# The image stage of a one-layer vision tower: side work in another order, decay references added by GpSimd, one exponential per slot

## The chip, the cores and the metric

The kernel runs on one core of a Trainium2 chip. The metric is the device time of one execution in microseconds. The time before is the median of three runs.

## What is computed

Sixteen images of 5x128x128 are cut into 256 patches each. A patch embedding (320 to 256) with a normalisation gives the tokens h; a gated decay attention with 16 heads of 64 adds to h; a mixture of 8 experts, two per token, adds again. The part that the change touches is the decay of the attention and the order of what is done beside it:

```
q, k = silu(x Wq), silu(x Wk);  v = x Wv;  gate = sigmoid(x Wg)
cum   = cumsum(-softplus(x Wa + ba), over the tokens of an image)
decay = exp(where(causal, cum_i - cum_j, -inf))        per head
o     = ((q k^T) * decay) v;  o = norm(o per head) * gn_w + gn_b
h     = h + (o * gate) Wo;    then norm, router, top 2, experts
```

## The kernel before, in words

The image stage works on pairs of images: eight pairs (p), and for each eight steps (c), one for every two heads. The five engines each have a program written out by hand, and `step(p, c)` of each lists what it does in that step. Besides the attention of pair p ("main"), a step holds side work of the neighbours: the embedding of pair p+1 ("nxt": `tokens`, `embed`, `embed_norm`, `turn`, `keep_xnT`, `decay_logits`, `softplus`, `log_decay`, `cum`, `running_sums`, `keep_cum`), the second half of the output projection and the second normalisation of pair p-1 ("post": `gn_mean`, `spread`, `gn_var`, `affine`, `affined`, `gated`, `y_hi`, `y_lo`, `out_proj`, `residual`, `normed`, `turn2`, `keep_x2`, `route`), and the sorting of pair p-2 into lists by expert ("routed": `choose`, `ranks`, `place`, `scatter`). Engines take their instructions strictly in the order written; semaphores join them.

The main work of a step on TensorE is: `scores` of image 0 (L883, L886), `queries` of the next step (L849), `weighted` of image 0 (L896, L900), `scores` of image 1, `keys` and `gates` of the next step (L849), `weighted` of image 1; the eight blocks of v are made by `values` (L842), spread over the steps. `gates(4)` waits until all eight blocks of v have been copied out of their PSUM banks by ScalarE's `keep_v` (L585). The last step of a pair also has the first half of the output projection (`out_proj`, L926).

Decay. The running sums are written to HBM and read back, broadcast to 128 partitions, into a ring of four slots (`dec_x`, 128x768 each: two heads of 384 columns; a slot is one image of one step). SyncE loads a slot (`load_decay`) when VectorE has used the slot four before it. GpSimd's `decay_rows` (L449) fills what is not causal with -1e30, one step ahead of its use; ScalarE's `decay` (L594) takes exp with the negative running sum `ncum` as the bias of a partition: four instructions a slot, because the bias differs by head and by block of rows. VectorE's `decayed` (L1197) multiplies the scores with it. GpSimd's other work is reciprocal roots by pow (`embed_rsqrt` L455, `group_rsqrt` L460, `row_rsqrt` L464) and `scatter`, eight indirect DMAs a pair (L471), four in step 3 and four in step 4. In `decay_rows` order before, a root or four indirect DMAs stand between the slot of image 0 and that of image 1.

After the image stage comes the expert stage: 39 blocks of 256 rows, whose code is not touched.

Of the kernel before, what the change touches and what calls it, by code (L numbers as in the profile page):

```python
# [65 lines left out]
def vit_layer(nc, xT, w_tok, gamma, wq, wk, wv, wg, wa, ba, wo, gn_w, gn_b,  # L66
# [3 lines left out]
    with ExitStack() as ctx:  # L70
# [88 lines left out]
        st = sb("st", [P, NS, 3])  # L159
        rs = sb("rs", [P, NS])  # L160
# [61 lines left out]
        dec_in0 dec_in1 dec_in2 dec_in3 causal exp_done  # L222
# [41 lines left out]
        def _(sp):  # L264
# [70 lines left out]
            for p in range(NPR):  # L335
                for c in range(NP):
                    if c == 6 and pair(p + 1):
                        store_cum(p + 1)
                    ahead(p, c, 0)
                    if pair(p + 1):  # L340
                        if c == 0:
                            load_patches(2 * p + 3)
# [4 lines left out]
                    if c == 2 and pair(p + 2):  # L347
# [85 lines left out]
        def _(pool):  # L433
# [9 lines left out]
            def decay_rows(p, c, u):  # L443

                n = 2 * NP * p + 2 * c + u
                pool.wait_ge(M[f"dec_in{n % RING}"], 16 * (n // RING + 1))
                for hh in range(2):
# [14 lines left out]
            def row_rsqrt(n):  # L462
                pool.wait_ge(M["b_ve"], n + 1)
                pool.tensor_tensor(rs[:, :], rs[:, :], mhalf[:, 0:NS], ALU.pow).then_inc(M["b_rs"], 1)  # L464
# [9 lines left out]
            for p in SPAN:  # L474
                for c in range(NP):
                    nc_p, nc_c = (p, c + 1) if c + 1 < NP else (p + 1, 0)
                    if pair(nc_p):
                        decay_rows(nc_p, nc_c, 0)
                    if c == 0 and pair(p + 1):
                        embed_rsqrt(2 * p + 2)  # L480
                    if c == 2 and pair(p + 1):
                        embed_rsqrt(2 * p + 3)
                    if c in (3, 4) and pair(p - 2):
                        scatter(p - 2, c - 3)
                    if c in (4, 5) and pair(p - 1):
                        row_rsqrt(2 * p - 2 + c - 4)
                    if pair(nc_p):
                        decay_rows(nc_p, nc_c, 1)
                    if c == 0 and pair(p - 1):
                        group_rsqrt(2 * p - 1)  # L490
                    if c == 5 and pair(p):
                        group_rsqrt(2 * p)
# [30 lines left out]
        def _(act):  # L523
# [63 lines left out]
            def decay(p, c, u):  # L587
                n = 2 * NP * p + 2 * c + u
                act.wait_ge(M["causal"], 2 * (n + 1))
                act.wait_ge(M["ncum_done"], p + 1)  # L590
                for hh in range(2):
                    for s, cols in ((0, slice(0, S)), (1, slice(S, LW))):
                        d = dec[n % RING][:, hh, cols]
                        act.activation(d, d, ACT.Exp, bias=ncum[p % 2][:, NS * u + s, 2 * c + hh:2 * c + hh + 1]).then_inc(M["exp_done"], 1)  # L594
# [32 lines left out]

            def step(p, c):
                main, nxt, post, routed = pair(p), pair(p + 1), pair(p - 1), pair(p - 2)
                if c == 7 and nxt:  # L630
                    xn_hi(p + 1)
                if main and c > 0:
                    keep_o(p, c - 1)
                if main and c + 1 < NP:
                    tanh_q(p, c + 1)
                    decay(p, c + 1, 0)
                if main:
                    if c == 0:
                        keep_v(p, 2, 2)
                        keep_v(p, 3, 1)  # L640
                    if c == 1:
                        keep_v(p, 4, 2)
                if nxt and c == 1:
                    keep_xnT(2 * p + 2)
                if post and c == 1:
                    affined(p - 1, 1, 0)
                if post and c == 2:
                    affined(p - 1, 1, 1)
                if main and c == 2:
                    keep_v(p, 6, 2)  # L650
                if main and c == 3:
                    keep_v(p, 7, 2)
                if post and c == 3:
                    y_hi(p - 1, 1, 1)
                if main and c == 6:
                    affined(p, 0, 0)
                if nxt and c == 6:
                    keep_cum(p + 1)
                if main and c + 1 < NP:
                    tanh_k(p, c + 1)  # L660
                if post and c == 6:
                    keep_x2(2 * p - 2)
                if main and c == 1:
                    keep_v(p, 5, 0)
                if main and c + 1 < NP:
                    decay(p, c + 1, 1)
                if main and c == 6:
                    affined(p, 0, 1)
                if nxt and c == 4:
                    softplus(p + 1)  # L670
                if main and c + 1 < NP:
                    tanh_g(p, c + 1)
                if nxt and c == 1:
                    scaled_h(2 * p + 2)
                if nxt and c == 3:
                    scaled_h(2 * p + 3)
                    keep_xnT(2 * p + 3)
                if routed and c == 1:
                    top_exp(2 * p - 4)
                    top_exp(2 * p - 3)  # L680
                if post and c == 2:
                    y_hi(p - 1, 1, 0)
                if post and c == 6:
                    keep_x2(2 * p - 1)
                if c == 7:
                    if nxt:
                        decay(p + 1, 0, 0)
                        tanh_q(p + 1, 0)
                        keep_v(p + 1, 0, 2)
                    if main:  # L690
                        y_hi(p, 0, 0)
                        keep_o(p, 7)
                    if nxt:
                        tanh_k(p + 1, 0)
                        keep_v(p + 1, 1, 0)
                    if main:
                        y_hi(p, 0, 1)
                    if nxt:
                        decay(p + 1, 0, 1)
                        tanh_g(p + 1, 0)  # L700
# [89 lines left out]
        def _(pe):  # L790
# [62 lines left out]
            def queries(p, c):  # L853
# [4 lines left out]
                have(pe, "v_done", 2 * TP * p + {1: 2, 3: 6}.get(c, 0))  # L858
# [9 lines left out]
            def gates(p, c):  # L868
# [3 lines left out]
                have(pe, "v_done", 2 * TP * p + {0: 1, 1: 3, 2: 5, 3: 7, 4: 8}.get(c, 0))  # L872
# [31 lines left out]
            def gn_mean(p, g):  # L904
                n = 2 * p + g
                have(pe, "h2a_done", 2 * p + 2 if g == 1 else 0)
                have(pe, "h2_done", 2 * p - 1 if g == 0 else 0)
# [3 lines left out]
            def gn_var(p, g):  # L911
                n = 2 * p + g
                have(pe, "h2_done", 2 * p if g == 0 else 0)
# [45 lines left out]
            def step(p, c):  # L959
                main, nxt, post, routed = pair(p), pair(p + 1), pair(p - 1), pair(p - 2)  # L960
                if main:
                    scores(p, c, 0)
                    if c + 1 < NP:
                        queries(p, c + 1)
                if main:
                    if c == 0:
                        values(p, 2, 2, "tg_done", NP * p + 1)
                        values(p, 3, 1, "sk_done", NP * p + 1)
                    if c == 1:
                        values(p, 4, 2, "tg_done", NP * p + 2)  # L970
                    if c == 2:
                        values(p, 6, 2, "tg_done", NP * p + 3)
                    if c == 3:
                        values(p, 7, 2, "tg_done", NP * p + 4)
                if c == 0 and post:
                    gn_mean(p - 1, 1)
                if c == 1 and nxt:
                    turn(2 * p + 2)
                if c == 3 and nxt:
                    turn(2 * p + 3)  # L980
                if c == 4 and nxt:
                    logits(p + 1)
                if c == 4 and post:
                    out_proj(p - 1, 1, 0, *(("taken_done", p - 1) if routed else ("gv_done", 2 * p)))
                if c == 5 and post:
                    out_proj(p - 1, 1, 1, *(("gt2_done", 2 * p + 1) if main else ("h2_done", 2 * p - 1)))
                if c == 6 and nxt:
                    cum_rows(p + 1)
                if c == 6 and post:
                    turn2(2 * p - 2, *(("gv_done", 2 * p + 1) if main else ("h2_done", 2 * p)))  # L990
                if c == 7:
                    if pair(p + 2):
                        tokens(2 * p + 4)
                    if post:
                        route(2 * p - 1)
                if main:
                    weighted(p, c, 0)
                    scores(p, c, 1)
                    if c + 1 < NP:
                        keys(p, c + 1)  # L1000
                if c == 0 and post:
                    gn_var(p - 1, 1)
                if c == 1:
                    if main:
# [590 lines left out]
```

## Time and profile before

| what | us |
|---|---|
| median of 3 runs (lowest, highest) | 1525.53 (1521.51, 1531.65) |
| the profiled execution's own time | 1527.12 |
| its span in the trace | 1525.3 |
| image stage in steady work, 48 to 970 us of the span | 922 |
| expert stage, from 1030 us | 495 |

The profile is of one execution. Busy times of an engine are unions of its instructions; a mean duration of a matmul holds its latency, so the time that a group of matmuls takes is read from the starts in the timeline.

### The profile page before, as it was taken

How to read it: one execution, taken by the hardware profiler on the slowest of the kernel's cores; microseconds unless marked ns; L12 is line 12 of the kernel's file. 1: busy time of each engine (PE TensorE's matmuls, PEld its weight loads, DVE VectorE, ACT ScalarE, POOL GpSimd, SP SyncE). 2: the span in 40 equal slices, each digit the busy share in tenths (PEclk: the TensorE clock that was granted, in tenths of full speed). 3: DMA queues.
4: the chain of work that ended last, by engine and by line, in shares of the span. 5: the costliest groups of instructions: out<-in, count | busy, mean ns of one | idle time of the engine just before them, and what ended most of it. 6: DMA issues, size and time to landing. Idle time of an engine off the chain costs nothing. (4 is left out here: it accounts for less than half of the span.)

```text
span 1525.3 us, 28980 instructions
## 1 busy us (share of the span) xinstructions
PE 1347.0 (88%) x9012; PEld 1132.2 (74%) x9012; DVE 923.7 (61%) x2290; ACT 933.9 (61%) x2197; POOL 462.0 (30%) x538
## 2 busy tenths in 40 slices
PE   4799899889889988989888899437999999999996
PEld 3566666667667766767767777437999999999996
DVE  3445454554554564465455555555888888888884
ACT  2557456456366365464555575306888888888884
POOL 2111112132132133124023223131444444444544
PEclk9999999999999999999999999658999999999999
DMA  5322123132132222223222223227777777777772
GB/s 188 95 71 103 50 85 92 50 103 82 61 94 70 82 79 83 83 68 105 70 70 97 74 84 98 76 75 240 218 224 216 221 227 238 230 233 220 214 228 61
DMA packets 126021, 192.86 MB, mean 126 GB/s; under 512 B 17216, under 2 KB 92192, under 8 KB 125792
## 3 DMA queue, kind: packets, MB, share of 16 engines
q1 hardware_dynamic: 111344, 174.52, 35.3%
q0 software_dynamic: 14592, 17.26, 5.2%
q8 instruction: 46, 0.75, 0.2%
q14 instruction: 39, 0.32, 0.1%
HBM read 166.01 MB, written 29.96 MB: 128 GB/s over the span
## 5 line engine op out<-in xcount | busy, mean ns | idle before, releaser
L849 PE MATMUL bank<-xn_sp,big_r 128*128 128x512 f32 x1152 | 316.6, 412 | 0.0
L594 ACT ACTIVATE dec_x<-dec_x,ncum 128x256 f32<-128x256 f32 (+1 forms) x512 | 190.2, 446 | 134.4 <-POOL dec_x L449 134.4
L849 PEld LDWEIGHTS bank<-xn_sp,big_r 128*128 128x128 f32 x1152 | 204.5, 190 | 55.2 <-issue 4.5
L1197 DVE TENSOR_TENSOR att<-bank,dec_x 128x384 f32<-128x384 f32 x256 | 130.7, 552 | 186.5 <-PE bank L886 176.4
L1073 PE MATMUL bank<-big_r 128*128 128x256 f32 x1872 | 239.0, 284 | 0.9 <-DVE big_r L1487 0.9
L1073 PEld LDWEIGHTS bank<-big_r 128*128 128x128 f32 x1872 | 231.9, 193 | 1.3 <-DVE big_r L1487 1.3
L1437 DVE TENSOR_TENSOR big_r<-big_f,big_r 128x512 fp32r<-128x512 f32 x236 | 162.6, 691 | 12.8
L743 ACT ACTIVATE mid_f<-bank,dec_x 128x256 f32<-128x256 f32 x312 | 145.0, 477 | 27.4 <-DVE big_r L1505 23.0
L502 POOL TENSOR_SCALAR mid_f<-mid_f,dec_x 128x256 f32<-128x256 f32 x78 | 91.0, 1172 | 227.0 <-DVE mid_f L1513 227.0
L1505 DVE TENSOR_TENSOR big_r<-mid_f,big_r 128x256 fp32r<-128x256 f32 x312 | 131.7, 422 | 39.5 <-ACT big_r L749 39.5
L449 POOL TENSOR_SCALAR_AFFINE_SELECT dec_x<-dec_x 128x256 f32<-128x256 f32 x256 | 103.7, 437 | 156.2 <-DMA dec_x<-cum_scratch 156.1
L729 ACT ACTIVATE big_r<-big_f 128x512 fp32r<-128x512 f32 x236 | 149.4, 636 | 0.0
L926 PE MATMUL bank<-big_r,y_sp 128*128 128x256 f32 x768 | 119.8, 323 | 33.2 <-DVE y_sp L1245 31.6
L926 PEld LDWEIGHTS bank<-big_r,y_sp 128*128 128x128 f32 x768 | 116.3, 231 | 38.0 <-issue 34.7
L508 POOL DMA_INDIRECT out<-mid_f,tok x78 | 128.4, 1646 | 47.7 <-POOL mid_f L502 30.6
L455 POOL TENSOR_TENSOR rs<-rs,mhalf 128x4 f32<-128x4 f32 x16 | 23.7, 1481 | 360.4 <-DVE rs L1132 360.4
L749 ACT ACTIVATE big_r<-mid_f 128x256 fp32r<-128x256 f32 x312 | 132.6, 425 | 0.0
L1085 PE MATMUL bank<-big_r 128*128 128x256 f32 x960 | 124.4, 286 | 0.0
L1085 PEld LDWEIGHTS bank<-big_r 128*128 128x128 f32 x960 | 119.2, 194 | 0.0
L1085 PE MATMUL bank<-y_sp,big_r 128*128 128x256 f32 x912 | 117.1, 285 | 0.0
L842 PE MATMUL bank<-big_r,xn_sp 128*128 128x512 f32 x384 | 100.2, 401 | 18.3 <-ACT big_f L578 18.3
L1085 PEld LDWEIGHTS bank<-y_sp,big_r 128*128 128x128 f32 x912 | 111.9, 192 | 0.0
(154 smaller groups left out, 1990.2 us busy)
## 6 DMA issues: line engine op xcount, KB each, us to landing
big_f<-in_L_ffn_w SPq DMA_DIRECT2D x78, 1024.0 KB, 6.5
dec_x<-cum_scratch SPq DMA_DIRECT2D x128, 384.0 KB, 3.5
mid_f<-expert_rows SPq DMA_DIRECT2D x39, 261.0 KB, 7.0
tq<-in_L_ffn_b SPq DMA_DIRECT2D x39, 128.0 KB, 2.9
xt<-in_x SPq DMA_DIRECT2D x16, 256.0 KB, 3.8
h_scratch<-h SPq DMA_DIRECT2D x16, 256.0 KB
h<-h_scratch SPq DMA_DIRECT2D x8, 512.0 KB, 4.3
out<-h SPq DMA_DIRECT2D x16, 256.0 KB, 4.0
```

What stands on the lines that cost most here:

```text
L508: pool.indirect_dma_start(out=out_rows, out_offset=bass.IndirectOffsetOnAxis(ap=tok[par][:, s:s + 1], axis=0), in_=yo[par][:, s, :], in_of ...
L594: act.activation(d, d, ACT.Exp, bias=ncum[p % 2][:, NS * u + s, 2 * c + hh:2 * c + hh + 1]).then_inc(M["exp_done"], 1)
L729: act.activation(parts[0].rearrange("p k n -> p (k n)")[:, cols], staged[par][:, cols], ACT.Copy).then_inc(M[f"{name}_hi"], 1)
L743: act.activation(gel[c % NGEL], bank[2 + c % HB][:, 0:BLK], ACT.Gelu_apprx_tanh, bias=b1_sb[par][:, c:c + 1]).then_inc(M["gel_done"], 1)
L749: act.activation(g_sp[0][:, c, :], gel[c % NGEL], ACT.Copy).then_inc(M["gh_done"], 1)
L849: mm = pe.matmul(bank[target][:, :], wp[:, k, c * P:(c + 1) * P], xp[:, k, :], start=(k == 0 and j == 0), stop=(k == EC - 1 and j == 2))
L926: mm = pe.matmul(bank[7][:, s * E:(s + 1) * E], yp[:, j, u * S + s * P:u * S + (s + 1) * P], wp[:, GC * g + j, :], start=(j == 0 and s == ...
L1073: mm = pe.matmul(bank[2 + c % HB][:, 0:BLK], wp[:, k, c * P:(c + 1) * P], xp[:, k, :], start=(k == 0 and j == 0), stop=(k == EC - 1 and j ...
L1085: mm = pe.matmul(bank[6 + s // 2][:, (s % 2) * E:(s % 2 + 1) * E], gp[:, c, s * P:(s + 1) * P], wp[:, c, :], start=(c == 0 and s % 2 == 0 ...
L1197: dve.tensor_tensor(att[hh][:, :], bank[4 + hh][:, 0:LW], dec[n % RING][:, hh, :], ALU.mult).then_inc(M["mult_done"], 1)
L1437: dve.tensor_tensor(lo, staged[par][:, cols], f32(hi), ALU.subtract).then_inc(M[f"{name}_lo"], 1)
L1505: dve.tensor_tensor(g_sp[1][:, c, :], gel[c % NGEL], f32(g_sp[0][:, c, :]), ALU.subtract).then_inc(M["gl_done"], 1)
```

## The change

It reorders the side work of all five engines' steps and moves the subtraction of the running sums from ScalarE's bias to GpSimd. The diff, cut to what the prediction speaks of:

```diff
 GpSimd
-            pool.wait_ge(dec_in); two affine_selects
+                pool.wait_ge(M["ncum_done"], p + 1)
+                for s, cols in ((0, slice(0, S)), (1, slice(S, LW))):
+                    d = dec[n % RING][:, :, cols]
+                    ref = ncum[p % 2][:, NS * u + s, 2 * c:2 * c + 2].rearrange(...).broadcast_to(d.shape)
+                    pool.tensor_tensor(d, d, ref, ALU.add).then_inc(M["shifted"], 1)
+                pool.wait_ge(M["shifted"], 2 * (n + 1))
...
+                    q, d = (p, c + 1) if c + 1 < NP else (p + 1, 0)
+                    if pair(q):
+                        decay_rows(q, d, 0)
+                        decay_rows(q, d, 1)
+                    if c == 0 and post:
+                        group_rsqrt(2 * p - 1)
+                    if c in (0, 2) and nxt:
+                        embed_rsqrt(2 * p + 2 + c // 2)
+                    if c in (2, 3) and routed:
+                        scatter(p - 2, c - 2)
+                    if c in (4, 5) and post:
                         row_rsqrt(2 * p - 2 + c - 4)
+                    if c == 5 and main:
                         group_rsqrt(2 * p)
 ScalarE
-                for hh in range(2):
-                    for s, cols in ((0, slice(0, S)), (1, slice(S, LW))):
-                        d = dec[n % RING][:, hh, cols]
-                        act.activation(d, d, ACT.Exp, bias=ncum[...]).then_inc(M["exp_done"], 1)
+                d = dec[n % RING].rearrange("p h n -> p (h n)")
+                act.activation(d, d, ACT.Exp).then_inc(M["exp_done"], 1)
 SyncE
                 for c in range(NP):
-                    if c == 6 and pair(p + 1):
-                        store_cum(p + 1)
-                    ahead(p, c, 0)
...
+                        if c == 2: store_h(2 * p + 2)
+                        if c == 4: store_h(2 * p + 3)
+                        if c == 6: store_cum(p + 1)
+                    ahead(p, c, 0)
```

The new order, by step (the instructions themselves stay, except as above):

- TensorE: step 0 `values` 2 and 3, `gn_mean`, `gn_var`; step 1 `values` 4, `ranks`, `turn`, `values` 5; step 2 `tokens(2p+3)` (was step 1), `values` 6 into bank 0 behind `keys` (was bank 2 behind `queries`); step 3 `values` 7, and `turn(2p+3)` behind `gates` (was ahead of `weighted`); step 4 `out_proj(p-1,1,0)` , `logits` behind `keys`, `out_proj(p-1,1,1)` behind `gates` (was step 5); step 5 `gn_mean(p,0)`, `gn_var(p,0)`, `turn2(2p-2)` (was step 6); step 6 `cum` (was step 5), `route(2p-2)`, `turn2(2p-1)`, `cum_rows`, `route(2p-1)` (was step 7); step 7 both `out_proj(p,0,.)` one behind the other at the end (a `gates` stood between them).
- ScalarE: `softplus` in step 5 (was 4); `keep_cum` first in step 7 (was step 6); `keep_xnT(2p+3)` at the head of step 4 (was the end of step 3); `keep_x2(2p-2)` at the head of step 6; in step 3 the order is `keep_o`, `tanh_q(4)`, `decay(4,0)`, `keep_v(7)`, `y_hi(p-1,1,1)`, `tanh_k(4)`, `decay(4,1)`, `scaled_h`, `tanh_g(4)`; in step 7 `decay(p+1,0,0)` stands behind `tanh_q` and `keep_v`.
- VectorE: in step 2 `decayed(2,0)`, `head_stats`, `silu_q(3)`, `place`, `decayed(2,1)`, `silu_k(3)`, `gated(p-1,1,1)`, `embed(2p+3)` (was near the head of step 2); `embed_norm(2p+3)` behind `silu_k(4)` in step 3; `residual(2p-1)` and both halves of `normed` a little earlier in the steps; `gated(p,0,0)` in step 6 (was 7) and `gated(p,0,1)` early in step 7.
- `rs` and `st` get two buffers, so that the rows of one image need not wait for the other.

## Rows read from the trace of the kernel before

**Rows 1.** The page, part 1: busy us, share of span, instructions.

```profile
PE 1347.0 (88%) x9012; PEld 1132.2 (74%) x9012; DVE 923.7 (61%) x2290; ACT 933.9 (61%) x2197; POOL 462.0 (30%) x538
```

**Rows 2.** Windows: stretch, length, busy of PE, PEld, DVE, ACT, POOL, clock, DMA.

```profile
48.00:970.00 922.00, 828.82 (x4944) 627.92 (x4943) 478.20 (x1196) 503.15 (x1135) 213.21 (x347) 0.96 0.26 83
1030.00:1525.00 495.00, 473.34 (x3900) 470.14 (x3900) 394.83 (x928) 399.14 (x1007) 219.38 (x156) 0.98 0.71 213
```

**Rows 3.** Waits of PE, 48 to 970 us: us in total, times, longest.

```profile
PE bank L926 <- DVE y_sp L1245: 24.8, 8, 3.9
PE bank L842 <- ACT big_f L578: 18.3, 7, 3.3
PE bank L896 <- DVE att L1197: 16.1, 13, 2.8
PE bank L818 <- ACT xs L530: 14.0, 5, 2.8
PE bank L944 <- ACT turned L618: 9.5, 7, 1.4
```

**Rows 4.** Waits of ACT, same stretch.

```profile
ACT dec_x L594 <- POOL dec_x L449: 134.4, 42, 6.2
```

**Rows 5.** Timeline of POOL in pair 3: start us, us, instructions [idle before].

```profile
413.05 1.01 POOL L455 TENSOR_TENSOR rs<-rs,mhalf 128x4 f32<-128x4 f32 x1 [30.14 <-DVE rs L1132]
...
439.22 1.93 POOL L455 TENSOR_TENSOR rs<-rs,mhalf 128x4 f32<-128x4 f32 x1 [20.57 <-DVE rs L1132]
...
447.07 1.03 POOL L471 DMA_INDIRECT expert_rows<-xn,slot  x1 [4.47 <-DVE slot L1330]
...
453.91 1.48 POOL L449 TENSOR_SCALAR_AFFINE_SELECT dec_x<-dec_x 128x256 f32<-128x256 f32 x4
```

**Rows 6.** Timeline of PE in pair 3.

```profile
423.60 3.34 PE L802 MATMUL bank<-wt,xt 128*128 128x256 f32 x12
...
428.45 0.65 PE L896 MATMUL bank<-att,mid_f 128*64 128x256 f32 x4
...
429.25 0.70 PE L883 MATMUL bank<-q_s,k_s 64*128 64x256 f32 x4
...
430.11 1.67 PE L849 MATMUL bank<-xn_sp,big_r 128*128 128x512 f32 x6
...
459.83 4.61 PE L926 MATMUL bank<-big_r,y_sp 128*128 128x256 f32 x24
...
472.85 3.03 PE L926 MATMUL bank<-big_r,y_sp 128*128 128x256 f32 x24
```

**Rows 7.** Groups by line and shape, whole span: busy us, mean ns, idle before.

```profile
L594 ACT ACTIVATE dec_x<-dec_x,ncum 128x256 f32<-128x256 f32 x256 | 128.4, 501 | 134.4 <-POOL dec_x L449 134.4
...
L449 POOL TENSOR_SCALAR_AFFINE_SELECT dec_x<-dec_x 128x256 f32<-128x256 f32 x256 | 103.7, 437 | 156.2 <-DMA dec_x<-cum_scratch 156.1
L594 ACT ACTIVATE dec_x<-dec_x,ncum 128x128 f32<-128x128 f32 x256 | 100.1, 391 | 0.0
L502 POOL TENSOR_SCALAR mid_f<-mid_f,dec_x 128x256 f32<-128x256 f32 x78 | 91.0, 1172 | 227.0 <-DVE mid_f L1513 227.0
...
L471 POOL DMA_INDIRECT expert_rows<-xn,slot x64 | 73.8, 1153 | 70.0 <-DVE slot L1330 53.8 <-issue 16.2
...
L571 ACT ACTIVATE tq<-bank 128x512 f32<-128x512 f32 x64 | 38.2, 596 | 118.1 <-PE bank L849 118.0
...
L612 ACT ACTIVATE y_sp<-big_f 128x1024 fp32r<-128x1024 f32 x32 | 33.6, 1050 | 4.4 <-DVE big_f L1239 4.4
```

**Rows 8.** Timeline of DVE in pair 3, an `embed` and what follows it.

```profile
436.43 0.70 DVE L1119 BATCH_NORM_STATS2 st<-bank 128x6 f32<-128x512 f32 x1 [3.30 <-DMA h_scratch<-h]
...
439.06 1.23 DVE L1239 SCALAR_TENSOR_TENSOR big_f<-big_f 128x1024 f32<-128x1024 f32 x1
...
441.14 0.68 DVE L1188 SCALAR_TENSOR_TENSOR k_s<-tq,bank 128x512 f32<-128x512 f32 x1
...
442.18 0.88 DVE L1140 TENSOR_SCALAR turned<-h,st1u,rs 128x256 f32<-128x256 f32 x2
```

More of the change, by code:

```diff
@@ L346, in _ @@
                             store_h(2 * p + 3)
-                    if c == 2 and pair(p + 2):
+                        if c == 6:
+                            store_cum(p + 1)
+                    ahead(p, c, 0)
+                    if c == 0 and pair(p + 1):
+                        load_patches(2 * p + 3)
+                    if c == 3 and pair(p + 2):
                         load_patches(2 * p + 4)
@@ L626, in top_exp, with last_step @@
                                    accum_out=tsum[:, t, :]).then_inc(M["tope_done"], 1)
+            def last_step(p):
+                main, nxt = pair(p), pair(p + 1)
+                if nxt:
+                    keep_cum(p + 1)
+                    xn_hi(p + 1)
+                if main:
+                    y_hi(p, 0, 0)
+                    keep_o(p, 6)
+                    y_hi(p, 0, 1)
+                if nxt:
+                    tanh_q(p + 1, 0)
+                    keep_v(p + 1, 0, 2)
+                    decay(p + 1, 0, 0)
+                if main:
+                    keep_o(p, 7)
+                if nxt:
+                    tanh_k(p + 1, 0)
+                    keep_v(p + 1, 1, 0)
+                    decay(p + 1, 0, 1)
+                    tanh_g(p + 1, 0)
@@ L635, in step @@
+                if main:
                     tanh_q(p, c + 1)
                     decay(p, c + 1, 0)
-                if main:
[L638 to L648, printed above, removed]
@@ L678, in step @@
-                if routed and c == 1:
+                    for i, source in {0: ((2, 2), (3, 1)), 1: ((4, 2),), 3: ((7, 2),)}.get(c, ()):
+                        keep_v(p, i, source)
+                if c in (1, 2) and post:
+                    affined(p - 1, 1, c - 1)
+                if c == 3 and post:
+                    y_hi(p - 1, 1, 1)
+                if c == 5 and nxt:
+                    softplus(p + 1)
+                if c == 6 and main:
+                    affined(p, 0, 0)
+                if main:
+                    tanh_k(p, c + 1)
@@ L679, in step @@
+                if c == 6 and post:
+                    keep_x2(2 * p - 1)
+                if main:
+                    decay(p, c + 1, 1)
+                    if c in (1, 2):
+                        keep_v(p, c + 4, 0)
+                if c == 0 and routed:
                     top_exp(2 * p - 4)
                     top_exp(2 * p - 3)
-                if post and c == 2:
+                if c == 1 and nxt:
+                    keep_xnT(2 * p + 2)
+                    scaled_h(2 * p + 2)
+                if c == 2 and post:
@@ L682, in step @@
                     y_hi(p - 1, 1, 0)
[L683 to L700, printed above, removed]
+                if c == 3 and nxt:
+                    scaled_h(2 * p + 3)
@@ L702, in start @@
+                if c == 6 and main:
+                    affined(p, 0, 1)
+                if main:
+                    tanh_g(p, c + 1)
             def start(c):
@@ L906, in gn_mean @@
                 have(pe, "h2a_done", 2 * p + 2 if g == 1 else 0)
-                have(pe, "h2_done", 2 * p - 1 if g == 0 else 0)
+                have(pe, "h2_done", 2 * p if g == 0 else 0)
                 pe.wait_ge(M["gst_done"], GC * (n + 1))
@@ L957, in ranks, with last_step @@
                 mm.then_inc(M["rk_ps"], 1)
-            def step(p, c):
-                main, nxt, post, routed = pair(p), pair(p + 1), pair(p - 1), pair(p - 2)
+            def last_step(p):
+                main, nxt = pair(p), pair(p + 1)
                 if main:
-                    scores(p, c, 0)
-                    if c + 1 < NP:
-                        queries(p, c + 1)
+                    scores(p, 7, 0)
+                if pair(p + 2):
+                    tokens(2 * p + 4)
                 if main:
[L966 to L1004, printed above, removed]
-                        values(p, 5, 0, "sq_done", NP * p + 3)
-                    if nxt:
-                        tokens(2 * p + 3)
-                if c == 2 and routed:
-                    ranks(p - 2, *(("gv_done", 2 * p) if post else ("taken_done", p - 2)))
-                if c == 4 and main:
-                    gn_mean(p, 0)
-                if c == 5:
-                    if main:
-                        gn_var(p, 0)
-                    if nxt:
-                        cum(p + 1)
-                if c == 6 and post:
-                    route(2 * p - 2)
-                if main and c + 1 < NP:
-                    gates(p, c + 1)
-                if c == 6 and post:
-                    turn2(2 * p - 1, "lg_done", 2 * p - 1)
-                if c < 7:
-                    if main:
-                        weighted(p, c, 1)
-                    return
@@ L1027, in step @@
+                    weighted(p, 7, 0)
+                    scores(p, 7, 1)
                 if nxt:
@@ L1331, in place, with last_step @@
                                          op0=ALU.mult, op1=ALU.add).then_inc(M["slot_done"], 1)
+            def last_step(p):
+                main, nxt, post = pair(p), pair(p + 1), pair(p - 1)
+                if main:
+                    decayed(p, 7, 0)
+                if post:
+                    keep_logits(2 * p - 1)
+                if main:
+                    gated(p, 0, 1)
+                if nxt:
+                    xn_lo(p + 1)
+                if main:
+                    head_stats(p, 6)
+                    y_lo(p, 0, 0)
+                    decayed(p, 7, 1)
+                if nxt:
+                    silu_q(p + 1, 0)
+                if main:
+                    y_lo(p, 0, 1)
+                if nxt:
+                    silu_k(p + 1, 0)
+                if post:
+                    choose(2 * p - 2)
+                if main:
+                    first_half(p, 0)
+                    first_half(p, 1)
@@ L1369, in step @@
-                if main and c == 7:
-                    gated(p, 0, 0)
+                if c == 2 and routed:
+                    place(p - 2)
+                if c == 3 and post:
+                    y_lo(p - 1, 1, 0)
+                if c == 5:
+                    if post:
+                        normed(2 * p - 2)
+                    if main:
+                        spread(p, 0)
+                if c == 6:
+                    if post:
+                        normed(2 * p - 1)
+                        keep_logits(2 * p - 2)
+                    if nxt:
+                        running_sums(p + 1)
```

250 lines of the change are left out of this document (124 added, 126 removed).

## The prediction, made before the changed kernel was run

> **What bounds the kernel now.** I read the page first, then the windows by stage, the waits of TensorE in the image stage, and then one pair (pair 3, 394 to 510 us) instruction by instruction. The page shows TensorE busy for 88% of the span, twice as long as GpSimd and well ahead of VectorE and ScalarE at 61% [rows 1]. The windows split this: the expert stage is 96% busy on TensorE (473.34 of 495 us) and is not touched; the image stage has 922 us with TensorE busy for 828.82 [rows 2]. So 93 us of idle time, about 12 us in each of eight pairs of 115.3 us, is all that a better order can win at the present speed of the matmuls. The waits name it: five of them hold 82.7 us [rows 3]. ScalarE and VectorE are busy for 55% and 52% of this stage [rows 2], so for them it is only lateness that counts, not length.
>
> Where the lateness comes from: ScalarE stands 134.4 us before the exponential, waiting for GpSimd's causal fill [rows 4]. GpSimd is late because its queue stands behind something else: at 439.22 it had waited 20.57 us for an `embed` before it could go on to the fill of image 1, and at 447 to 454 us four indirect DMAs stood between two fills [rows 5].
>
> **The change, part by part.** Times are on the clock of TensorE, from the start of a step. From the starts in the trace: `weighted` 0.80, `scores` 0.86, one projection or block of v 1.5, `tokens` 3.3, an `out_proj` 3.0 us at full clock [rows 6]; ScalarE 0.60 for 512 columns, 1.05 for 1024 [rows 7]; VectorE 1.2 for `gated`, 2.6 from the start of `embed` to its last statistic, 0.7 for a silu, 0.8 for `embed_norm` [rows 8].
>
> Exponential. Four instructions of 2x501 and 2x391 ns are 1.78 us of durations for a slot; one of 768 columns without bias lies between 596 ns for 512 and 1050 for 1024 columns, so 0.82 us [rows 7]. For 128 slots that is 123 us less on ScalarE. ScalarE is 45% idle, so I count nothing for it by itself: the matmuls hide it. If the cover is gone, it is worth 1 us wherever ScalarE is what is late.
>
> GpSimd's additions: 128x512 and 128x256 for a slot. The trace has no such instruction. The fill costs 437 ns for 256 columns, so three times that, 1.3 us, is the low end; L502, one operation of arithmetic on 256 columns, costs 1172 ns, so 3.5 us is the high end [rows 7]. I take 2.4 us, midway, as two instructions carry less fixed cost than three. With the two fills a slot then costs 3.2 us, and two slots 6.4 of a step of 14.4 on average. GpSimd's load rises by 16 x 2.4 = 38 us a pair, to 65 of 115 us (27 now [rows 2]): not a bound, but it matters wherever GpSimd starts late.
> The Trainium skill (GPSIMD Engine Reference, Elementwise — side-by-side cycle accounting) gives about 2.6 cycles of 1.2 GHz a column for an addition of two tensors, by which the additions would be 1.7 us a slot, and the stall below 0.7 us shorter. No run here shows it yet.
>
> Order, what goes. `gated(p,0,0)` moves from step 7 to 6, so the second `y_lo` is ready before `out_proj`: the 24.8 us go; both `out_proj` now stand next to each other, and the second waits some 0.9 us for `first_half` (0.7 us and the signals), 7 us in eight pairs. Both fills precede the roots, so `tanh_g` of step 0 is not late for `values(4)`: the 18.3 us go. `store_h` is issued before a wait on the scores and `embed(2p+3)` comes late in step 2, so the wait for its DMA (3.30 us [rows 8]) and with it the 16.1 us go. `keep_xnT` at the head of step 4 and `logits` behind `keys`: the 14.0 us go. `turn2` a step earlier and `keep_x2` at the head of step 6: the 9.5 us go. All by [rows 3]. `store_cum` now waits for `keep_cum`, first in step 7; the decay of the next pair lands some 8 us later, is added and filled by 12, and exp, `tanh_k` and `silu_k` are done by 14 to 15 of the 21 us of step 7: hidden, with 6 us to spare, and what SyncE has queued behind it (`store_h2`, `load_h`) is wanted at 17.
>
> Order, what is late next. Step 2 on TensorE: `scores` 0.9, `queries` 2.4, `tokens` 5.7, `weighted` 6.5, `scores` 7.4, `keys` 8.9, `values(6)` 10.4, `gates` 11.9, `weighted` 12.7. On VectorE `silu_k(3)` is done at 8.9+0.6+0.7 = 10.2, `gated` at 11.4, and `embed(2p+3)` at 14.1, that is 1.4 us into step 3. GpSimd waits for exactly this in `embed_rsqrt`, takes 1.0 us and goes on to four indirect DMAs: 73.8+16.2 us for 64 are 1.4 each [rows 7], 5.6 us. So it turns to slot (4,0), long landed, at 8.1, and has it added and filled at 11.3. ScalarE, in order, stands before that exponential: done at 12.1, `keep_v(7)` at 12.7. `gates(4)` needs that copy and could have begun at 7.1: a stall of 5.6 us. Behind it `y_hi`, `tanh_k`, `silu_k` and `embed_norm` follow at 13.7, 14.3, 15.0 and 15.8, while `turn(2p+3)` is wanted at 14.2: 1.6 more. Together 7.2 us in each pair that has both a next pair and one to scatter, p = 2 to 6, five times: 36 us. Pairs 0 and 1 have no scatter: slot (4,0) is ready at 5.7, and only `turn` is 0.5 late. Pair 7 has no `embed`.
> Step 5 has 8.8 us of matmuls, and `spread`, `softplus` with its table loads and `affine` all in it: `gn_var` and `turn2` together wait some 1.5 us. Step 6 finds its slots 3.4 and 6.6 us in, and nothing waits.
>
> Clock. After a 2.8 us gap an `out_proj` took 4.61 us where another took 3.03 [rows 6]: a dip costs 1.6. Now I count one dip a pair beyond the idle time; with the longer gap in step 3 I take 1.5 dips for pairs 2 to 6, 2.4 us.
>
> Sum. TensorE's 828.82 us of work are 103.6 a pair, 102.0 without the dip; with 11.7 idle that makes the 115.3 [rows 2]. (By my step lengths, 11.3, 12.4, 12.7, 9.9, 15.6, 8.8, 10.9 and 20.2 us, it is 101.8.) Pairs 2 to 6 after: 102.0+7.2+1.5+0.9+2.4 and 0.5 for small waits = 114.5, a gain of 0.8 each, 4 us. Pairs 0, 1 and 7: the gaps of 9 to 10 us and a dip shrink to about 3; 8, 9 and 5 us (pair 7 has less beside it). The tail, where `scatter` now precedes the roots: 1 us. Together 27 us: the profiled execution's 1527.1 would be 1500, and the median, which lies 1.6 us lower, 1498.5.
>
> **The rivals.** *The stall in step 3 isn't there* or is covered. For it: the chain has eight links that I timed, and a few us of slack on any would do. Against: GpSimd stood behind the same scatter before [rows 5]. Time: 1498.5-36 = 1462.5.
> *VectorE and GpSimd hold each other up.* For it: the pow at 439.22 took 1.93 us, the same at 413.05 took 1.01; a `gated` with both inputs in SBUF had begun at 439.06 and ended at 440.29 [rows 5, 8]. That a pow of 1.0 us ended 0.9 late fits. VectorE has 9 such instructions of some 1.2 us a pair, and GpSimd's additions now fill 38 of 115 us: a third meet, for up to a us each. If 2.5 us a pair land on the path, the time is 1498.5+20 = 1518.5. Against: most have slack.
> The Trainium skill (SBUF — State Buffer, Who interferes with whom) says that a VectorE instruction with two SBUF inputs and a GpSimd instruction that reads SBUF exclude each other for the whole instruction; the trace agrees in the row of 1.93 us.
> *GpSimd becomes what sets the pace* (the other side). If the additions cost 4.5 us a slot, a slot is 5.3. Then step 3 stalls 2.1 more, in step 6 the second slot is filled at 10.8, `tanh_g` comes at 14, `keep_cum` behind it holds `tokens` in step 7 for 2.7, and other steps give 0.7: 5.5 a pair, 44 us, 1542. It decides from about 3.7 us for the additions of a slot, where the 27 us of gain are gone. For it: L502 at 1172 ns for 256 columns comes near, and that with one tensor as input [rows 7]. Against: the fill costs a third of it.
>
> **How the numbers follow.** Forecast 1498.5, in 1480 to 1510: 0.42. No stall, 1455 to 1480: 0.20. Holding each other up, 1510 to 1530: 0.22. GpSimd sets the pace, over 1530: 0.16. A measurement of this kernel tells about 1% from no change, here 1510.3 and 1540.8. Faster by over 1%: 0.62; within: 0.26; slower: 0.12. The range, 1462 to 1540, leaves out a tenth at either end.
>
> **What would show it.** Right: waits of TensorE for `y_sp`, `xs` and `turned` nearly gone; one wait of L849 for `mid_f` (L585) of some 5 us in pairs 2 to 6 only; ScalarE's exponentials near 0.8 us; additions near 1.6 and 0.8 us; pairs 0 and 1 near 106 us, pairs 2 to 6 near 114. Wrong: additions over 3 us for 512 columns; no wait of `gates(4)`; or pairs 0 and 1 no shorter than now.

## The result, and the profile after

The kernel with the change takes 1462.64 us (median of four, 1459.87 to 1465.48); the kernel before, run beside it, 1528.59. The ratio is 0.956, with a 95% interval of 0.950 to 0.963: 4.4% faster. Forecast were 1498.5 us and a gain of 27; it was 66, more than twice that, and the time is just inside the lower end of the stated range. The direction held and the size did not. Between the two profiled executions, whose spans are 1525.3 and 1463.6 us, the gain is 61.7.

The page of the kernel after, part 1, answers to [rows 1]:

```profile
PE 1317.6 (90%) x9012; PEld 1117.6 (76%) x9012; DVE 951.7 (65%) x2290; ACT 857.2 (59%) x1813; POOL 667.2 (46%) x794
```

The same 9012 matmuls are busy for 29 us less than before (1347.0). Nothing in the change makes a matmul cheaper, and this row alone says that something besides waiting went. ScalarE has 77 us less, GpSimd 205 more, and VectorE, with the same 2290 instructions, 28 us more.

Windows of the kernel before (columns as in [rows 2]): from the first scores to the first `out_proj` of the last pair, and from there to the experts, and the experts:

```profile
54.20:962.44 908.24, 815.84 (x4895) 617.39 (x4894) 476.26 (x1185) 501.42 (x1131) 211.67 (x343) 0.96 0.25 80
962.44:1030.69 68.25, 27.84 (x144) 25.69 (x144) 32.65 (x148) 13.88 (x36) 19.74 (x19) 0.60 0.25 84
1030.69:1525.30 494.61, 473.34 (x3900) 470.14 (x3900) 394.83 (x928) 399.14 (x1007) 219.38 (x156) 0.98 0.71 213
```

and of the kernel after:

```profile
54.20:900.28 846.08, 789.14 (x4900) 604.98 (x4899) 504.54 (x1185) 425.46 (x751) 413.94 (x603) 0.98 0.27 86
900.28:967.35 67.07, 25.54 (x144) 23.50 (x144) 32.57 (x148) 14.34 (x37) 20.99 (x19) 0.62 0.26 89
967.35:1463.60 496.25, 474.84 (x3900) 471.59 (x3900) 394.87 (x928) 399.55 (x1007) 219.79 (x156) 0.98 0.71 212
```

The image stage is 62.2 us shorter; the other two come to nothing together. Of the 62.2, TensorE's idle time gives 35.5 (92.4 to 56.9) and its busy time 26.7 (815.8 to 789.1), at a granted clock that rises from 0.96 to 0.98 (1.00 is 2.4 GHz, and 0.50 the lower level of 1.2 GHz).

The waits of TensorE in the kernel after, 0 to 920 us, answer to [rows 3]:

```profile
PE bank L844 <- ACT mid_f L589: 26.7, 7, 5.2
...
PE bank L920 <- DVE h L1246: 13.0, 8, 2.5
...
PE bank L931 <- DVE gr L1217: 4.3, 6, 0.7
PE bank L891 <- ACT big_f L600: 4.0, 2, 2.5
PE bank L891 <- DVE att L1192: 2.9, 2, 1.5
```

All five old waits are gone or down to 3 us. Two new ones stand in their place: `gates(4)` for the copy of v, and the second `out_proj` for `first_half`. The first is the predicted stall. It is 5.2 us in each of pairs 2 to 6; what is left of the 26.7 us, in two other pairs, is under 0.5 us a time. GpSimd's timeline in pair 3 shows its cause: the root, then four indirect DMAs, and only then slot (4,0):

```profile
411.52 1.02 POOL L461 TENSOR_TENSOR rs<-rs,mhalf 128x4 f32<-128x4 f32 x1 [12.01 <-DVE rs L1127]
412.72 1.03 POOL L477 DMA_INDIRECT expert_rows<-xn,slot  x1 [0.18 <-issue]
...
418.24 1.61 POOL L451 TENSOR_TENSOR dec_x<-dec_x,ncum 128x512 f32<-128x512 f32 x2
419.92 0.77 POOL L455 TENSOR_SCALAR_AFFINE_SELECT dec_x<-dec_x 128x256 f32<-128x256 f32 x2
```

ScalarE then, and TensorE behind it:

```profile
420.72 0.84 ACT L595 ACTIVATE dec_x<-dec_x 128x768 f32<-128x768 f32 x1 [7.75 <-POOL dec_x L455]
421.47 0.58 ACT L589 ACTIVATE mid_f<-bank 128x512 f32<-128x512 f32 x1
```

```profile
415.31 1.67 PE L844 MATMUL bank<-xn_sp,big_r 128*128 128x512 f32 x6
422.20 2.90 PE L844 MATMUL bank<-xn_sp,big_r 128*128 128x512 f32 x6 [5.22 <-ACT mid_f L589]
425.03 0.80 PE L806 MATMUL bank<-ident,turned 128*128 128x128 f32 x4
```

Look at the second of these rows: six matmuls of the same shape take 1.67 us before the wait and 2.90 behind it. The windows of these two groups show the lower clock itself, 1.00 before the wait and 0.50 behind it:

```profile
415.31:416.90 1.59, 1.59 (x8) 1.04 (x6) 1.02 (x2) 0.00 (x0) 1.28 (x2) 1.00 0.97 352
422.20:425.03 2.83, 2.83 (x6) 1.84 (x7) 1.51 (x4) 2.07 (x4) 2.29 (x5) 0.50 0.09 32
```

What the clock costs before and after is the term that the prediction got most wrong.

### The profile page after: what moved, and what is told of

It reads as the page before. It is cut to its first block and busy times, and to the rows that moved or that the text cites. A ratio compares the mean times of both kernels' runs of the same rounds, so it can differ in the third digit from the quotient of the medians.

```text
span 1463.6 us, 28844 instructions
## 1 busy us (share of the span) xinstructions
PE 1317.6 (90%) x9012; PEld 1117.6 (76%) x9012; DVE 951.7 (65%) x2290; ACT 857.2 (59%) x1813; POOL 667.2 (46%) x794
## 5 line engine op out<-in xcount | busy, mean ns | idle before, releaser
L844 PE MATMUL bank<-xn_sp,big_r 128*128 128x512 f32 x1152 | 322.5, 417 | 26.7 <-ACT mid_f L589 26.7
L451 POOL TENSOR_TENSOR dec_x<-dec_x,ncum 128x512 f32<-128x512 f32 (+1 forms) x256 | 214.5, 859 | 130.3 <-DMA dec_x<-cum_scratch 130.0
L844 PEld LDWEIGHTS bank<-xn_sp,big_r 128*128 128x128 f32 x1152 | 209.5, 193 | 84.1 <-issue 31.8
L595 ACT ACTIVATE dec_x<-dec_x 128x768 f32<-128x768 f32 x128 | 107.5, 840 | 85.0 <-POOL dec_x L455 84.0
L570 ACT ACTIVATE tq<-bank 128x512 f32<-128x512 f32 x64 | 38.3, 598 | 175.6 <-PE bank L844 175.6
L920 PE MATMUL bank<-big_r,y_sp 128*128 128x256 f32 x768 | 101.2, 290 | 23.4 <-DVE h L1246 13.0
L920 PEld LDWEIGHTS bank<-big_r,y_sp 128*128 128x128 f32 x768 | 98.5, 196 | 27.3 <-DVE h L1246 14.6
L1080 PE MATMUL bank<-y_sp,big_r 128*128 128x256 f32 x912 | 117.1, 285 | 0.0
L1183 DVE SCALAR_TENSOR_TENSOR k_s<-tq,bank 128x512 f32<-128x512 f32 x64 | 44.0, 688 | 106.8 <-ACT tq L575 106.8
```

Source lines behind the costliest of these rows:

```text
L451: pool.tensor_tensor(d, d, ref, ALU.add).then_inc(M["shifted"], 1)
L844: mm = pe.matmul(bank[target][:, :], wp[:, k, c * P:(c + 1) * P], xp[:, k, :], start=(k == 0 and j == 0), stop=(k == EC - 1 and j == 2))
L920: mm = pe.matmul(bank[7][:, s * E:(s + 1) * E], yp[:, j, u * S + s * P:u * S + (s + 1) * P], wp[:, GC * g + j, :], start=(j == 0 and s == ...
L1080: mm = pe.matmul(bank[6 + s // 2][:, (s % 2) * E:(s % 2 + 1) * E], gp[:, c, s * P:(s + 1) * P], wp[:, c, :], start=(c == 0 and s % 2 == 0 ...
```

## The experiments

Two kinds of theory stand against each other in the expectations. The clock theory: a wait of a few us costs its length and then again, as the matmuls behind it run at the lower clock; the order removes waits and so earns twice, and the decay arithmetic is hidden. Its rivals: the shorter queue of ScalarE earns a part; or waits cost only their length.

**Order alone, arithmetic alone.** In `order_only` GpSimd's additions are out and the four exponentials with bias are in again; `decay_only` is the kernel before with the opposite edit:

```diff
 order_only, against the kernel after (decay_only: the reverse, in the old order)
-                    pool.tensor_tensor(d, d, ref, ALU.add).then_inc(M["shifted"], 1)
-                pool.wait_ge(M["shifted"], 2 * (n + 1))
...
-                act.activation(d, d, ACT.Exp).then_inc(M["exp_done"], 1)
+                for hh in range(2):
+                    for s, cols in ((0, slice(0, S)), (1, slice(S, LW))):
+                        act.activation(dec..., ACT.Exp, bias=ncum...).then_inc(M["exp_done"], 1)
```

> The new order of all engines with the old decay: four exponentials of a slot with bias, no additions on GpSimd. The clock theory (the order takes away waits of TensorE, and with them the slow matmuls behind them; the decay arithmetic is hidden): the stall of gates(4) in pairs 2 to 6 falls from 5.2 to 4.2 us, because a slot costs GpSimd 1.6 us less and ScalarE 0.65 more; TensorE's busy time in the image stage stays at 789 us; 1457 us, in 1450 to 1464. The rival, that the 76 us less on ScalarE are worth something by themselves: 1475 or more.

> The old order with the new decay: additions on GpSimd and one exponential of 768 columns. The clock theory: all five old waits of TensorE stay, and those behind GpSimd (for tg and xs) grow by 1 us each, so 12 us slower than before, 1535 to 1545 us, with TensorE busy for 816 us or more in the image stage. The rival, that the arithmetic brings a part of the gain: 1500 to 1520 us.

Measured: `order_only` 1464.7 us (1453.55 to 1465.92), as fast as the kernel after; `decay_only` 1606.45 (1601.86 to 1611.44), ratio 1.051 (1.043 to 1.059), 78 us slower than before. All of the gain is the order's. The arithmetic, which costs nothing measurable here in the new order, costs 5% in the old. The median of `order_only` is 1 us outside its range, and the stall of `gates(4)` is 4.2 us, as expected. For `decay_only` my figure of 12 us missed by six times. TensorE's busy time did what the clock theory says: 810.5 us in `order_only` beside 814.9 in the kernel after, and 879.4 in `decay_only` beside 843.9 before (table below, from 54 us to the first matmul of the experts).

**The exponential or the additions?** `exp_only_old` is `decay_only` without the additions. It leaves out the subtraction of the running sums.

> The old order with one exponential of 768 columns per slot, and no additions on GpSimd: it leaves out the subtraction of the running sums. The theory that the additions are what made decay_only 78 us slower, because two or three slots queue behind each root in GpSimd and each comes 1.6 us later: about as before or a little faster, 1515 to 1530 us. The rival, that waiting for a whole slot in one instruction does it: 1560 us or more.

Measured: 1523.64 us (1520.0 to 1527.5), ratio 0.996 (0.994 to 0.998). So 76 us less on ScalarE are worth some 6 us, and the additions, 1.6 us a slot, cost 83 in the old order. GpSimd's timeline in `decay_only` shows how 1.6 us grow. Four slots and another root stand behind one root:

```profile
570.16 1.02 POOL L461 TENSOR_TENSOR rs<-rs,mhalf 128x4 f32<-128x4 f32 x1 [27.65 <-DVE rs L1135]
571.15 1.61 POOL L451 TENSOR_TENSOR dec_x<-dec_x,ncum 128x512 f32<-128x512 f32 x2
...
573.56 1.65 POOL L466 TENSOR_TENSOR gr<-gr,mhalf 128x8 f32<-128x8 f32 x1
575.18 1.61 POOL L451 TENSOR_TENSOR dec_x<-dec_x,ncum 128x512 f32<-128x512 f32 x2
...
577.67 1.64 POOL L451 TENSOR_TENSOR dec_x<-dec_x,ncum 128x512 f32<-128x512 f32 x2
...
580.11 1.61 POOL L451 TENSOR_TENSOR dec_x<-dec_x,ncum 128x512 f32<-128x512 f32 x2
```

In a queue of slots each is late by its own addition and by those ahead of it, the fourth by 6.4 us. ScalarE waits 236.6 us for GpSimd there, against 134.4 [rows 4].

**The stall in step 3, removed.**

```diff
-                    if c in (2, 3) and routed:
-                        scatter(p - 2, c - 2)
+                    if c in (3, 4) and routed:
+                        scatter(p - 2, c - 3)
```

> The kernel after, with both scatters one step later, behind the two slots of that step. The clock theory: the 26 us of wait for keep_v(7) go, and the slow matmuls behind them, 1.4 us in each of five pairs, go as well: 1430 us, TensorE busy 782 us in the image stage. Rival one, only the waits go and the busy time stays: 1437 us. Rival two, the next link (turn behind embed_norm, or normed behind the later scatter) takes the place of the stall: 1445 us or more.

Measured: 1435.17 us (1432.49 to 1438.49), 27 us faster than the kernel after and between the theory's 1430 and the 1437 of rival one. The wait of `gates(4)` fell from 26.7 to 2.1 us, and `turn` now waits for `embed_norm`, 8.5 us in seven pairs, which the stall had covered. Idle time fell by 19.0 us, less than the 26 expected because of `turn`, and busy time by 10.9, where rival one has it stay: the matmuls behind the stall ran fast again.

**A wait put back.** `late_y` is the kernel after with `gated(p,0,0)`, `y_hi` and `y_lo` late in step 7, as in the old order:

```diff
 VectorE (gated(p, 0, 0) out of step 6; last_step:)
+                    gated(p, 0, 0)
...
                     decayed(p, 7, 1)
                     silu_q(p + 1, 0)
+                    y_lo(p, 0, 0)
+                    gated(p, 0, 1)
                     silu_k(p + 1, 0)
+                    y_lo(p, 0, 1)
```

> The kernel after, with the gating of the first half, y_hi and y_lo put back late in step 7, as in the old order. The 2.98 us wait for y_sp comes back in eight pairs, the 1.9 us wait between the two out_proj becomes 0.8. The clock theory: 9 to 17 us of idle time and 1.57 us for each first out_proj at the lower clock, together 1484 us, and TensorE busy 800 us or more in the image stage. The rival, that a wait costs its own length and no more: 1472 us, busy 789.

Measured: 1490.82 us (1486.24 to 1492.04), 28 us slower than the kernel after and 7 above the theory's figure, idle time 18.6 and busy time 9.4 us more. Of the five waits that the new order takes away, this is the only one that was put back by itself. The first `out_proj` and the second of one pair, in the timeline of `late_y`:

```profile
489.93 4.59 PE L924 MATMUL bank<-big_r,y_sp 128*128 128x256 f32 x24 [2.36 <-DVE y_sp L1244]
495.30 3.13 PE L924 MATMUL bank<-big_r,y_sp 128*128 128x256 f32 x24 [0.78 <-DVE h L1250]
```

In the kernel after, the same group takes 3.13 us behind an idle stretch of 1.94 and 4.54 behind one of 2.52:

```profile
481.75 3.13 PE L920 MATMUL bank<-big_r,y_sp 128*128 128x256 f32 x24 [1.94 <-DVE h L1246]
...
704.05 4.54 PE L920 MATMUL bank<-big_r,y_sp 128*128 128x256 f32 x24 [2.52 <-DVE h L1246]
```

The windows of these four groups give the clock beside the time, first those of `late_y`, then those of the kernel after:

```profile
489.93:494.50 4.57, 4.57 (x24) 4.38 (x24) 3.67 (x10) 0.14 (x1) 4.42 (x8) 0.63 0.02 4
495.30:498.30 3.00, 3.00 (x24) 2.92 (x24) 0.00 (x0) 0.00 (x0) 0.00 (x0) 1.00 0.00 0
```

```profile
481.75:484.80 3.05, 3.05 (x24) 2.92 (x24) 0.00 (x0) 0.00 (x0) 0.17 (x1) 1.00 0.00 0
704.05:708.50 4.45, 4.45 (x24) 4.24 (x24) 0.00 (x0) 0.00 (x0) 0.17 (x1) 0.64 0.02 4
```

So not every wait brings the lower clock, and in these rows those of 2.36 and 2.52 us did and that of 1.94 did not. One table for all kernels; its last column is TensorE's busy time in each half microsecond times the clock granted in it, added up, that is, what the busy time would be at full clock:

| kernel | stage, us | TensorE busy | idle | busy at full clock |
|---|---|---|---|---|
| decay_only | 1056.0 | 879.4 | 176.6 | 800.1 |
| before | 976.7 | 843.9 | 132.8 | 802.9 |
| double_add | 957.0 | 830.4 | 126.6 | 792.0 |
| exp_only_old | 974.4 | 850.0 | 124.4 | 801.9 |
| late_y | 941.4 | 824.3 | 117.1 | 793.6 |
| after | 913.4 | 814.9 | 98.5 | 792.1 |
| order_only | 903.1 | 810.5 | 92.7 | 791.4 |
| scatter_later | 883.5 | 804.0 | 79.5 | 793.1 |
| both | 883.8 | 805.5 | 78.3 | 792.8 |
| order_both | 871.2 | 801.1 | 70.1 | 790.2 |
| choose_late | 869.0 | 801.2 | 67.8 | 791.6 |

The matmuls are the same in all rows. From the bottom to the top idle time grows by 108.8 us and busy time by 78.2, 0.7 us for each us of waiting. It is no law: `exp_only_old` has 8.4 us less idle time than before and 6.1 more busy. The last column says what the growth is. In the eight kernels with the new order it is 790.2 to 793.6 us, while their busy time goes from 801.1 to 830.4: all of that spread is the granted clock. In the three with the old order it is 800.1 to 802.9, against 843.9 to 879.4. Between the two orders about 10 us remain that aren't the clock; the section on the prediction shows where most of them are.

**Gates between the two `out_proj`.**

```diff
-                    gates(p + 1, 0)
                     out_proj(p, 0, 0, "lg_done", 2 * p)
+                    gates(p + 1, 0)
                     out_proj(p, 0, 1, "h2a_done", 2 * p + 1)
```

`both` has this edit and the later scatter; `order_both` has both edits on `order_only`.

> scatter_later, and in step 7 the gates of the next pair stand between the two out_proj again. The wait of the second out_proj for first_half (13.6 us in eight in scatter_later) goes, as 1.5 us of other matmuls cover it: 1435 less 12 = 1423 us. Rival: VectorE's late choose, held up by GpSimd's additions, makes the same 13 us wait elsewhere: 1435 us.

> The same as both, with the old decay (four exponentials with bias, no additions on GpSimd). The theory that the arithmetic is only moved between engines with room, and that the additions cost something only by holding VectorE up: 1415 to 1423 us, VectorE busy for 30 us less than in both. The rival, that once the other waits are gone ScalarE's 76 us more show: 1430 us or more.

Measured: `both` 1433.6 us (1432.56 to 1435.27), no better than without the edit, with 12.0 us of the wait still there, so the rival's figure held and mine of 1423 did not; `order_both` 1421.42 (1419.24 to 1422.36), inside its range, with 0.8 us of it, in one pair. The 1.5 us of other matmuls should have covered a `first_half` of 0.7. That it didn't with the additions and did without them points at VectorE, which stands in `choose` just before. The group of its `pick` instructions in `order_only`, and in the kernel after:

```profile
L1290 DVE TENSOR_SCALAR pick<-iota,idxf 128x8 f32<-128x8 f32 x64 | 10.5, 233 | 0.3
```

```profile
L1293 DVE TENSOR_SCALAR pick<-iota,idxf 128x8 f32<-128x8 f32 x64 | 20.6, 389 | 0.3
```

and one `choose` of the kernel after in VectorE's timeline, with what GpSimd does then, additions and fills without a pause:

```profile
478.72 2.39 DVE L1293 TENSOR_SCALAR pick<-iota,idxf 128x8 f32<-128x8 f32 x4
481.02 0.68 DVE L1246 TENSOR_TENSOR h<-bank,h 128x512 f32<-128x512 f32 x1
```

```profile
477.05 1.61 POOL L451 TENSOR_TENSOR dec_x<-dec_x,ncum 128x512 f32<-128x512 f32 x2
478.73 0.77 POOL L455 TENSOR_SCALAR_AFFINE_SELECT dec_x<-dec_x 128x256 f32<-128x256 f32 x2
479.46 1.61 POOL L451 TENSOR_TENSOR dec_x<-dec_x,ncum 128x512 f32<-128x512 f32 x2
```

Four instructions on eight columns take 2.39 us there, where four took 0.62 us in the kernel before. The Trainium skill (SBUF — State Buffer, Who interferes with whom) has VectorE's `tensor_scalar` among the operations that can take the port pair shared with GpSimd, and a holder keeps it for a whole instruction; the trace agrees with that, though it doesn't show the port. VectorE is busy 507 us in the stage of `order_only` and 537 in that of the kernel after.

To tell it from a wait that merely moved, `choose` goes behind both `first_half`:

```diff
+                    first_half(p, 0)
+                    first_half(p, 1)
                 if post:
                     choose(2 * p - 2)
-                if main:
-                    first_half(p, 0)
-                    first_half(p, 1)
```

> The kernel both, with choose behind the two first_half in VectorE's step 7. The theory that GpSimd's additions stretch choose (small instructions that each wait for an addition) and so hold up first_half, and that this is all of the 12 us between both and order_both: the 12.0 us wait of the second out_proj goes, 1421 to 1425 us. Rival: the stretched choose is then in the way of the next decayed or of another wait, 1433 us or more.

Measured: 1418.11 us (1413.92 to 1421.19), ratio 0.928 (0.924 to 0.931): 15 us less than `both`, 3 below the range, and the fastest of all. The wait for `first_half` is down to 0.8 us in one pair. The 64 `pick` are back at a mean of 226 ns, so in its new place `choose` doesn't meet the additions at all: the edit took it out of `first_half`'s way and took away its slowness, and doesn't say which of the two counts. With the additions in, the kernel is as fast as `order_both` without them; the two ran on different chips, and `choose_late` without the additions wasn't run, so a few us between them are not excluded.

**How near is GpSimd to setting the pace?** `double_add` has two additions of zero more on each slot:

```diff
+                for cols in (slice(0, S), slice(S, LW)):
...
+                    pool.tensor_tensor(d, d, none, ALU.add).then_inc(M["shifted"], 1)
```

> The kernel after, with two more additions of zero on every slot (GpSimd 1.65 us a slot longer, 210 us in all, two signals more). The theory that only the slots behind a root or a scatter count: the wait of gates(4) grows from 5.2 to 6.9 in five pairs, 8 us, first_half comes later for another 5 to 10, slow matmuls behind these 5, and little else: 1480 to 1487 us. Rival one, GpSimd is fully covered but for gates(4): 1471 us. Rival two, GpSimd begins to set the pace: 1510 us or more.

Measured: 1507.43 us (1504.26 to 1513.89), 45 us slower than the kernel after and 20 above the theory's range. The wait of `gates(4)` went from 26.7 to 40.7 us and that of the second `out_proj` from 13.0 to 20.5; busy time rose by 15.5 us, with none of it left at full clock. The time lies between the theory's figure and that of rival two, and nearer the latter. Idle time rose by 28, of which these two waits are 21.5; two more, of `tokens` for the copy of the running sums (L804, 2.0 to 6.9 us) and of `gn_var` (L916, 0.9 to 3.5), hold the rest. So one more pair of additions a slot is no longer hidden. ScalarE waited for GpSimd 215.6 us, against 84.0.

**Order and arithmetic once more, side by side.**

> The kernel after once more, beside order_again on one chip: 1460 to 1466 us.

> order_only once more, on the same chip as after_again. Its six runs lay in two groups, 1454 to 1456 and 1464 to 1466 us. The clock theory: the groups differ in the granted clock and not in the work. Against after_again: between 0 and 10 us faster, with 8 us less of idle time from the two waits that the additions lengthen. The rival, that the exponential without bias is worth something in the new order: after_again is the faster one.

Measured: 1461.5 us (1459.83 to 1467.01) and 1456.16 (1453.13 to 1465.14). The runs of `order_again` at a mean clock of 0.966 and 0.967 took 1453 us, those at 0.963 to 0.959 took 1459 to 1465, as the clock theory has it. In the kernel after a few us between runs don't follow the mean clock: its run at 0.961 took 1459.87 us and one at 0.964 took 1465.48. The medians differ by 5 us and the runs overlap, so in the new order the arithmetic is worth nothing or costs a little.

## Why the prediction was right and wrong

*What bounds the kernel.* Right: TensorE's waits in the image stage, fed by lateness of GpSimd and ScalarE; 76 us less on ScalarE earned little or nothing by themselves (`order_only`, `exp_only_old`). (TensorE's 1347 us of busy time are nearly three times GpSimd's 462, not twice; nothing rests on this.)

*The exponential*, 0.82 us: 0.84. *The additions*, 2.4 us: the two take 1.61 back to back. The low end from the fill, 1.3, was nearer than the row of L502. The Trainium skill (GPSIMD Engine Reference, Elementwise — side-by-side cycle accounting) leads to an estimate of 1.7; the measurement has 1.61.

*The waits that go*: all five, as listed, but for 3 us of `weighted`. *The stall in step 3*: 5.6 us in pairs 2 to 6 was foreseen, 5.2 was measured in just these; the chain of eight links, timed by hand from rows, held. Its appendix, 1.6 us for `turn`, did not show: `gates(4)` ran 1.2 us longer at the lower clock and covered it. I had priced both. *`first_half`*, 0.9 us: 1.9, against 0.8 in `order_only`, by VectorE held up in `choose`. The rival on this was right in kind: but it named large instructions with two inputs in SBUF, where small ones were on the path, and its price of 2.5 us a pair is more than twice these 1.1. *Step 5*, 1.5 us: 0.22 and 0.71. *Pairs*: 106 us for pairs 0 and 1 (105.6 and 106.3 measured), 114 for 2 to 6 (110.4 to 111.8).

*The step that failed* is TensorE's busy time, and in it the clock: "Now I count one dip a pair beyond the idle time; with the longer gap in step 3 I take 1.5 dips for pairs 2 to 6, 2.4 us", on a base of "103.6 a pair, 102.0 without the dip". By this the busy time of the stage would be 1 us less after than before. It was 26.7 less: 15.7 by the clock and 11.0 in work at full clock.

The clock first. In one full pair of before, 391.68 to 510.93 us, not one but two `out_proj` ran at the lower clock: the one of 459.83 us in [rows 6], which follows a `decay_logits` that had waited, and the one at the pair's start, the first `out_proj` of step 7:

```profile
391.68 4.57 PE L926 MATMUL bank<-big_r,y_sp 128*128 128x256 f32 x24 [2.98 <-DVE y_sp L1245]
...
458.02 1.97 PE L818 MATMUL bank<-wa_sb,xs 128*128 128x16 f32 x16 [2.80 <-ACT xs L530]
```

By the half-microsecond sum the lower clock cost 3.4 us in that pair, two dips and not one. In the same pair after, 371.32 to 481.75 us, it cost 1.6, for the one dip behind the stall, where I had 2.4. Over the stage, 54.20 us to the first `out_proj` of the last pair, it cost 31.0 us before and 15.3 after. I had added to the dips for the longer gap in step 3, and had not taken off those that would go with the waits for `xs` and `y_sp`.

Then the base. I divided 828.82 us by eight for a full pair; but the first and last pairs have less beside them. The same pair, before:

```profile
391.68:510.93 119.25, 105.97 (x640) 80.41 (x640) 63.38 (x166) 64.75 (x147) 30.11 (x46) 0.97 0.25 82
```

That is 13.3 us idle and not 11.7, and 4.2 us of busy time beyond the 101.8 that my own step lengths gave. With the clock's 3.4 us taken off, the pair has 102.6 us of work before and 100.6 after; I had put this difference at nothing. Most of it is in `weighted`, which did not run in one piece where `decayed` was late. Here its eight matmuls take 1.17 us (the `scores` behind it start at 442.07), where 0.80 is usual, and the difference counts as busy:

```profile
440.90 0.80 PE L896 MATMUL bank<-att,mid_f 128*64 128x256 f32 x3 [1.97 <-DVE att L1197]
441.35 0.38 PE L900 MATMUL bank<-att,mid_f 128*64 128x128 f32 x2
```

In that pair `weighted` (L896 and L900, after L891 and L895) is busy for 18.2 us before and 16.6 after, while the mean duration of one of its matmuls is the same within 1 ns. So a part of what looks like work is waiting, too.

Pair by pair, all of the 35 us by which the gain between the profiled executions exceeded the forecast lie in pairs 2 to 6: 119.0 us a pair before and 111.2 after, a gain of 7.8 where I had 0.8. Of the 7.0, 4.3 are busy time and 2.7 idle time. For pairs 0, 1 and 7 together I had 22 us, and they gave 23; but that is luck, as pair 0 gave 1, not 8, and pair 7 gave 11.5, not 5.

*The rival* in which the stall is not there named the right time (1462.5 us) for the wrong reason: the stall was there. That the measured time falls on it is chance.

## What to carry to other kernels

Price a wait of a TensorE-bound stage by its length and by the matmuls that follow it at the lower clock. Look up in the trace in how many places of one full period the clock falls, and which of them go with the waits that the change removes. Check the busy time of one full period against the sum of its matmuls before dividing a stage by its periods. A change that loads an in-order queue is free only where nothing is queued behind a late instruction: the same 1.6 us a slot cost 83 us in one order and at most a few in the other. Before giving GpSimd elementwise work, look at what small VectorE instructions run beside it and who waits for them.

## What was not expected of the hardware

Four VectorE `tensor_scalar` instructions of eight columns took 2.39 us beside GpSimd's additions, 0.62 us without. A busy time of the same 5040 matmuls that ranged from 801 to 879 us, and from 790 to 803 once multiplied by the granted clock. And one kernel on one chip (`order_again`) whose runs lay 12 us apart with the mean granted clock, 0.967 to 0.959.
